# Transposing the second layernorm's output by DMA instead of on TensorE, in a fused cross-attention and FFN kernel

## The reference

```python
def _layernorm(x, axis=-1, eps=1e-05):
    m = jnp.mean(x, axis=axis, keepdims=True)
    v = jnp.var(x, axis=axis, keepdims=True)
    return (x - m) / jnp.sqrt(v + eps)

# xattn(u, ctx): q = Wq u, k = Wk ctx, v = Wv ctx (b, c, positions)
#   softmax(q^T k / sqrt(C)) over the 256 columns, times v, plus Wskip u
# ffn(u): w = (nibbles(qweight) - round(zeros / scales)) * scales, 1024 x 1024
#   y = u @ w + bias
x = x + xattn(_layernorm(x), ctx)        # 32 x 128 x 1024, float32
x = x + ffn(_layernorm(x))               # contraction over the 1024 positions
```

## Time and profile before

| | |
|---|---|
| median of 3 runs | 616.7 us (616.62 to 617.56) |
| the profiled execution's own time | 616.67 us |
| its span, first to last instruction | 614.8 us |
| TensorE busy | 588.1 us (96%) |
| VectorE busy | 476.5 us (77%) |
| GpSimd busy | 468.7 us (76%) |
| ScalarE busy | 409.4 us (67%) |
| granted TensorE clock, mean | 0.989 of full |
| transfers | 41.4 MB, the queue of SyncE 19.7% of 16 engines |

### The profile page before, as it was taken

The page is one execution under the profiler, slowest core; times in us unless marked ns, Lnnn a source line. Parts: engine busy times, 40 slices in busy tenths (PEclk is TensorE's granted clock), DMA queues, the critical chain, the costliest instruction groups (busy, mean ns, idle before and its releaser), DMA issues.

```text
span 614.8 us, 10932 instructions
## 1 busy us (share of the span) xinstructions
PE 588.1 (96%) x3348; PEld 416.1 (68%) x3348; DVE 476.5 (77%) x1027; ACT 409.4 (67%) x976; POOL 468.7 (76%) x520
## 2 busy tenths in 40 slices
PE   2868999999999999999999999999999999999996
PEld 2755777667777766777776677777677777667763
DVE  6787877878887777888778788878777877887762
ACT  4874677666668766666876666686666677666650
POOL 2453788777879877777977787897778789777866
PEclk9977999999999999999999999999999999999999
DMA  8011012222111222211222211122221112221002
GB/s 315 3 43 43 27 53 79 77 77 73 40 53 66 77 77 77 70 41 47 73 77 77 77 65 46 43 77 77 77 77 54 57 43 77 77 77 68 19 19 102
DMA packets 20178, 41.38 MB, mean 67 GB/s; under 512 B 2496, under 2 KB 7104, under 8 KB 20160
## 3 DMA queue, kind: packets, MB, share of 16 engines
q1 hardware_dynamic: 19584, 41.03, 19.7%
q10 hardware_dynamic: 576, 0.14, 0.1%
HBM read 24.39 MB, written 16.78 MB: 67 GB/s over the span
## 4 chain that ended last, share of the span: by engine, by line
PE 91%; DVE 5%; ACT 2%; issue 1%; DMA 1%; POOLq 0%; POOL 0%; ACTq 0%
PE ps_y L676 36%; PE ps_e L610 17%; PE ps_o L644 14%; PE ps_t L625 9%; PE ps_o L637 7%; PE ps_t L657 5%; PE ps_kv L688 2%; PE ps_kv L686 2%; DMA sb_x<-in_x_dram 1%; DVE sb_nib L457 1%; ACT sb_prob L288 1%; DVE sb_pt_lo L408 1%; DVE sb_neg_max L398 0%; ACT sb_pt_hi L297 0%; DVE sb_zp L499 0%
## 5 line engine op out<-in xcount | busy, mean ns | idle before, releaser
L288 ACT ACTIVATE sb_prob<-ps_e,sb_neg_max 128x256 f32<-128x256 f32 x256 | 118.7, 470 | 128.9 <-DVE sb_neg_max L398 128.8
L676 PE MATMUL ps_y<-sb_wf,sb_xnt_hi 128*128 128x512 f16 x512 | 196.1, 383 | 0.9 <-DVE sb_xnt_lo L448 0.9
L676 PE MATMUL ps_y<-sb_wf,sb_xnt_lo 128*128 128x512 f16 x512 | 194.0, 379 | 0.0
L214 POOL TENSOR_SCALAR sb_prob<-sb_prob,sb_rsum 128x256 f32<-128x256 f32 x256 | 117.7, 477 | 27.5 <-DVE sb_rsum L403 27.5
L408 DVE TENSOR_TENSOR sb_pt_lo<-ps_t,sb_pt_hi 128x512 fp32r<-128x512 f32 x128 | 88.3, 691 | 34.6 <-ACT sb_pt_hi L297 30.4
L398 DVE TENSOR_REDUCE sb_neg_max<-ps_e 128x2 f32<-128x512 f32 x128 | 87.7, 686 | 34.8 <-PE ps_e L610 34.8
L610 PE MATMUL ps_e<-sb_kv_hi,sb_xc_hi 128*128 128x256 f32 x256 | 91.6, 358 | 7.7 <-DVE sb_kv_lo L535 4.0
L297 ACT ACTIVATE sb_pt_hi<-ps_t 128x512 fp32r<-128x512 f32 x128 | 76.3, 598 | 33.9 <-PE ps_t L625 33.9
L676 PEld LDWEIGHTS ps_y<-sb_wf,sb_xnt_hi 128*128 128x128 f16 x512 | 49.7, 97 | 59.2 <-issue 17.6
L223 POOL TENSOR_TENSOR sb_rstd<-sb_ve,sb_neg_half 128x1 f32<-128x1 f32 x32 | 17.5, 548 | 92.3 <-DVE sb_ve L443 92.3
L250 POOL TENSOR_TENSOR sb_xc_lo<-sb_xc,sb_xc_hi 128x1024 fp32r<-128x1024 f32 x32 | 76.5, 2390 | 9.2 <-ACT sb_xc_hi L343 7.5
(11 more groups left out here) (85 smaller groups left out, 1162.9 us busy)
## 6 DMA issues: line engine op xcount, KB each, us to landing
sb_x<-in_x_dram SPq DMA_DIRECT2D x32, 512.0 KB, 3.3
out_dram<-sb_o SPq DMA_DIRECT2D x64, 256.0 KB, 2.1
sb_ctx<-in_ctx_dram SPq DMA_DIRECT2D x32, 128.0 KB, 2.5
sb_q<-in_L_ffn_qweight_dram SPq DMA_DIRECT2D x4, 512.0 KB, 6.4
sb_scale_row<-in_L_ffn_scales_dram SPq DMA_DIRECT2D x1, 512.0 KB, 8.7
sb_bias_row<-in_L_ffn_bias_dram SPq DMA_DIRECT2D x1, 512.0 KB, 9.5
sb_wk<-in_L_xattn_Wk_dram SPq DMA_DIRECT2D x1, 64.0 KB, 3.4
sb_wq<-in_L_xattn_Wq_dram SPq DMA_DIRECT2D x1, 64.0 KB, 3.3
```

Of the source, the lines that this page charges most:

```text
L214: last = pool.tensor_scalar(prob[:, j, t, :], prob[:, j, t, :], rsum[:, j, t:t + 1], 1.0, ALU.mult, ALU.mult)
L288: done = act.activation(prob[:, j, t, :], ps_e[j % 2][:, t, :], ACT.Exp, bias=neg_max[:, j, t:t + 1], accum_out=esum[:, j, t:t + 1])
L676: last = pe.matmul(ps_y[h][:, :], xnt_p[s][:, kt, :], wf[:, kt, h * HALF:(h + 1) * HALF], start=kt == 0 and s == 0, stop=kt == KT - 1 and ...
```

## The change

The transposes on TensorE (transpose_xn) are taken out. The split in two fp16 halves is made in SBUF before the transposition: ScalarE copies xn as fp16 to xn_hi with the columns in the order of the blocks (split_xn, one 1024-column instruction after probs_hi(1)), VectorE subtracts it from xn to xn_lo (split_xn_lo, one instruction after probs_lo(1)). SyncE then issues two DMA transposes a batch from SBUF to SBUF, 128 x 1024 fp16 each, into xnt_hi and xnt_lo, which get a second buffer. They stand in SyncE's step behind the stores and before the load of ctx. ffn(p, 0, 0) waits for both; the wait before its third quarter is gone. SyncE's stream is written out in full instead of looped; split_xn and split_xn_lo wait for the transposes of the batch before (xnt_loaded), and the first transpose waits for the FFN of the batch two before (y_done[1]). In the diff, cut to its core, the parts are in this order: buffers, SyncE, ScalarE, VectorE, TensorE; the calls of the removed and added functions follow from the order given above.

```diff
-        xnt_hi, xnt_lo = (sb(n, [P, KT, P], F16) for n in ("xnt_hi", "xnt_lo"))
+        xn_hi, xn_lo = (sb(n, [P, KT, P], F16) for n in ("xn_hi", "xn_lo"))
+        xnt_hi, xnt_lo = (sb(n, [P, 2, KT, P], F16) for n in ("xnt_hi", "xnt_lo"))
...
+                if ran(p):
+                    sp.wait_ge(xnhi_done, p + 1)
+                    if ran(p, 2):
+                        sp.wait_ge(y_done[1], p - 1)
+                    sp.dma_start_transpose(xnt_hi[:, 1 - par, :, :], xn_hi[:, :, :].rearrange(
+                        "c k r -> c (k r)")).then_inc(xnt_loaded[1 - par], 16)
+                    sp.wait_ge(xnlo_done, p + 1)
+                    sp.dma_start_transpose(xnt_lo[:, 1 - par, :, :], xn_lo[:, :, :].rearrange(
+                        "c k r -> c (k r)")).then_inc(xnt_loaded[1 - par], 16)
...
-            def xn_hi(p, h):
-                act.wait_ge(xnt_done[h], p + 1)
-                if h == 0 and ran(p, 1):
-                    act.wait_ge(y_done[1], p)
-                act.activation(xnt_hi[:, 4 * h:4 * h + 4, :], ps_t[h][:, :].rearrange("p (k r) -> p k r", r=P),
-                               ACT.Copy).then_inc(xnthi_done[h], 1)
+            def split_xn(p, par):
+
+                act.wait_ge(xn_done, p + 1)
+                if ran(p, 1):
+                    act.wait_ge(xnt_loaded[1 - par], arrived(p - 1, 1 - par, 32))
+                act.activation(xn_hi[:, :, :].rearrange("c (t e) r -> c t e r", e=2),
+                               xn[:, :].rearrange("c (t r e) -> c t e r", e=2, r=P),
+                               ACT.Copy).then_inc(xnhi_done, 1)
...
+            def split_xn_lo(p, par):
+
+                dve.wait_ge(xnhi_done, p + 1)
+                if ran(p, 1):
+                    dve.wait_ge(xnt_loaded[1 - par], arrived(p - 1, 1 - par, 32))
+                dve.tensor_tensor(xn_lo[:, :, :].rearrange("c (t e) r -> c t e r", e=2),
+                                  xn[:, :].rearrange("c (t r e) -> c t e r", e=2, r=P),
+                                  xn_hi[:, :, :].rearrange("c (t e) r -> c t e r", e=2),
+                                  ALU.subtract).then_inc(xnlo_done, 1)
...
-            def transpose_xn(b, p, h):
-
-                pe.wait_ge(xn_done, p + 1)
...
-                if g == 2 and h == 0:
-                    pe.wait_ge(xntlo_done[1], c + 1)
...
                     if h == 0:
-                        pe.wait_ge(xntlo_done[0], c + 1)
+                        pe.wait_ge(xnt_loaded[cpar], arrived(c, cpar, 32))
```

More of the change, by code:

```diff
@@ L127, in xattn_ffn_program @@
         nb2_done, xn_done = sem("nb2"), sem("xn")
-        xnt_done, xnthi_done, xntlo_done = sems("xnt", HALVES), sems("xnthi", HALVES), sems("xntlo", HALVES)
+        xnhi_done, xnlo_done, xnt_loaded = sem("xnhi"), sem("xnlo"), sems("xnt_loaded", 2)
         zpt_done, addbias_done, rest_done = sem("zpt"), sem("addbias"), sem("rest")
@@ L168, in step @@
             def step(b, par):
-                c = b - 3
+                c, p = b - 3, b - 1
                 if ran(c):
@@ L182, in step @@
                     sp.dma_start(x_sb[:, par, :], x[b + 2, :, :]).then_inc(x_loaded[par], 16)
-            run_steps(sp, step)
+            for b in range(-1, B + 3):
+                step(b, b % 2)
             for par in range(2):
@@ L320, in step @@
                     if ran(p, 1):
-                        act.wait_ge(xnt_done[1], p)
+                        act.wait_ge(xnlo_done, p)
                     act.activation(xn[:, :], x1[:, 1 - par, :], ACT.Identity, bias=nb2[:, :],
@@ L329, in step @@
                     probs_hi(b, 1)
+                if ran(p):
+                    split_xn(p, 1 - par)
                 if isinstance(b, int) and b in (0, 1):
@@ L354, in step @@
                                    scale=rs2[:, :]).then_inc(zpt_done, 1)
-                if ran(p):
-                    xn_hi(p, 0)
-                    xn_hi(p, 1)
                 if ran(n):
@@ L525, in finish @@
                     stats2(b, par, 0)
-                if ran(p):
-                    xn_lo(p, 0)
-                    xn_lo(p, 1)
                 if ran(n):
@@ L573, in step @@
                     probs_lo(b, 1)
+                if ran(p):
+                    split_xn_lo(p, 1 - par)
                 if isinstance(b, int) and b == 1:
@@ L620, in transpose_probs @@
                     pe.wait_ge(ptlo_done[j + 2], b)
-                if j < 2 and ran(b, 2):
-                    pe.wait_ge(xntlo_done[j], b - 1)
                 for m in range(MT):
@@ L646, in attend, with ffn @@
                 last.then_inc(attn_done[h], 1)
-            def transpose_xn(b, p, h):
-                pe.wait_ge(xn_done, p + 1)
-                if ran(b):
-                    pe.wait_ge(ptlo_done[2 + h], b + 1)
-                else:
-                    pe.wait_ge(xntlo_done[h], p)
-                for k in range(4):
-                    t, e = (4 * h + k) // 2, k % 2
-                    last = pe.transpose(ps_t[h][:, k * P:(k + 1) * P],
-                                        xn[:, 2 * P * t + e:2 * P * (t + 1):2], ident[:, :])
-                last.then_inc(xnt_done[h], 1)
-            def ffn(c, h, g):
+            def ffn(c, cpar, h, g):
                 if g == 0:
                     if h == 0:
-                        pe.wait_ge(xntlo_done[0], c + 1)
+                        pe.wait_ge(xnt_loaded[cpar], arrived(c, cpar, 32))
                     if ran(c, 1):
                         pe.wait_ge(prod_done[h], c)
-                if g == 2 and h == 0:
-                    pe.wait_ge(xntlo_done[1], c + 1)
                 if isinstance(c, int) and c == 0 and h == 0:
@@ L675, in ffn @@
                     for s in range(2):
-                        last = pe.matmul(ps_y[h][:, :], xnt_p[s][:, kt, :], wf[:, kt, h * HALF:(h + 1) * HALF],
+                        last = pe.matmul(ps_y[h][:, :], xnt_p[s][:, cpar, kt, :], wf[:, kt, h * HALF:(h + 1) * HALF],
                                          start=kt == 0 and s == 0, stop=kt == KT - 1 and s == 1)
@@ L700, in step @@
                 if ran(q):
-                    ffn(q, 0, 2)
+                    ffn(q, par, 0, 2)
                 if ran(b):
@@ L704, in step @@
                 if ran(q):
-                    ffn(q, 0, 3)
+                    ffn(q, par, 0, 3)
                 if isinstance(b, int) and b == 0:
@@ L710, in step @@
                 if ran(q):
-                    ffn(q, 1, 0)
+                    ffn(q, par, 1, 0)
                 if ran(b):
@@ L716, in step @@
                 if ran(q):
-                    ffn(q, 1, 1)
+                    ffn(q, par, 1, 1)
                 if ran(b):
@@ L720, in step @@
                 if ran(q):
-                    ffn(q, 1, 2)
+                    ffn(q, par, 1, 2)
                 if ran(b):
@@ L725, in step @@
                 if ran(q):
-                    ffn(q, 1, 3)
+                    ffn(q, par, 1, 3)
                 if ran(b):
@@ L732, in step @@
                     keys_values(n, 1 - par)
-                if ran(p):
-                    transpose_xn(b, p, 0)
                 if ran(b):
                     skip(b, par, 1)
-                if ran(p):
-                    transpose_xn(b, p, 1)
                 if ran(b):
@@ L741, in step @@
                 if ran(p):
-                    ffn(p, 0, 0)
-                    ffn(p, 0, 1)
+                    ffn(p, 1 - par, 0, 0)
+                    ffn(p, 1 - par, 0, 1)
             run_steps(pe, step)
```

4 lines of the change are left out of this document (removed).

## The result

The changed kernel takes **695.15 us** (median of 4 runs, 694.37 to 696.36) against 616.66 us for the kernel before: ratio 1.1275, 95% interval 1.1251 to 1.1299. That is 78.5 us slower, where 607 was forecast; the range ended at 690.

What follows compares the result with a forecast made beforehand. TensorE was taken as the bound, busy 588.1 of 614.8 us, with VectorE's queue taking back most of the gain. A step gains 0.06 + 0.27 = 0.33 us: 616.7 - 32 x 0.33 + 1 = 607 us, range 588 to 690.

Steps and rivals of the forecast that it cites:

- Steps 1 and 3: ScalarE's split_xn takes 1.06 us; on VectorE two products, probs_lo(2) and residual(0) queue behind split_xn_lo, until 304.08.
- Step 2: VectorE's split_xn_lo, 1024 columns, takes 1.23 us by a slope per column; bounds 0.7 and 2.3 us.
- Step 4: TensorE's skip(b, 1) starts 0.16 us later, plus 0.25 after the stall, less 0.47: 0.06 us earlier, not 0.94.
- Step 5: Lighter VectorE work behind brings the first row maximum 0.6 us earlier; TensorE's 0.27 us wait for the exponentials goes.
- Step 6: The two DMA transposes, 1.3 us fixed plus 1.1 us service each, land 2.4 us before ffn(b-1, 0, 0) and cost nothing.
- Rivals B and C: Before ffn(b-1, 0, 0): B, transposes land late, 645 us at 3 us service, chance 0.22; C, they bound, 1010 us, 0.12.
- Step 7: On SyncE's queue the context load stands behind the transposes, the x load waits for residual(1); both cost nothing.
- Step 8: In the last batch nothing covers the new path from xn to the products: about +1 us.
- Rival D: On VectorE split_xn_lo takes 2.3 us from its every-other-column read, passed straight to skip(b, 1): 641 us; chance 0.08.
- Rival A: As forecast, VectorE's queue takes back most of the gain: 607 us, its own range 588 to 614; chance 0.47.

Runs made afterwards that it cites:

- e2: The changed kernel with one added wait: GpSimd's bias addition waits until split_xn_lo is done; 609.83 us.
- e6: The changed kernel with 16 matmuls of 256 columns, whose result nobody reads, in TensorE's wait before skip(b, 1); 661.95 us.
- e5: The changed kernel with GpSimd's bias addition waiting for split_xn_lo and VectorE's two FFN products moved behind the first statistics; 605.59 us.
- e7: The changed kernel with GpSimd's bias addition waiting for split_xn_lo, one product ahead of the last row maximum, the other behind the first statistics; 604.94 us.
- e4: The changed kernel with each DMA transpose issued twice, one of them into a spare tile; 700.07 us.
- e1: The changed kernel with both splits taking the columns in plain order instead of every other column; 695.77 us.
- e12: The kernel before, transposes on TensorE, with VectorE's two products spread out and wsk_lo's subtraction moved behind variance2; 608.03 us.

## Why the prediction was wrong

The forecast was 607 us, the result 695. The working, step by step:

- **Steps 1 and 3, the queues: right.** split_xn takes 1141 ns for 1.06 us. From the end of split_xn_lo to x1 the forecast had 304.08 - 301.58 = 2.50 us; in the trace 315.85 to 318.26 is 2.41.
- **Step 2, the price of split_xn_lo: this is the step that failed.** It went by a slope per column, 1.23 us, with bounds of 0.7 and 2.3. The slope was right (1225 ns in e2, all 32 times), but in the changed kernel the instruction takes 2890 on average, above the upper bound, because both bounds came from what VectorE does alone. The rows used for the slope read one input from PSUM and one from SBUF, and the new instruction reads SBUF twice. With whom it would run side by side on GpSimd was never asked.
- **Step 4, the wait at skip(b, 1): place right, size wrong, one term missing.** Forecast was a wait of 0.4 to 0.9 us, 32 times. It is 2.4 us, in every batch; without the hold 0.7, as forecast. The 0.25 us for the stall was right too: skip(b, 1) takes 0.96 us for 0.70 where the clock is kept. What the sum put at nothing, without a reason, is what a longer wait does to TensorE's clock: e6 shows 33 us in all.
- **Step 5, the exponentials: right for this order.** Their wait is one of 3.2 us, and no longer 31; without the hold (e2) it is 5.2 us in 14 times for 18.5 in 31. It comes back when a product stands behind the statistics (19.3 us in e5 and e7).
- **Step 6, the transposes: right, a little dear.** Landing 3.1 us for the 2.4 forecast, SyncE held 1.24 us by each, 3 us to spare. Part of these 3 us is the delay of the reader: without the hold, in e2, the second is issued at 316.31, lands at 319.5 and is read at 321.10, so 1.6 us are left for the 2.4 forecast. The service: q1 took 30.0% of 16 x 693.4 us, against 19.7% of 16 x 614.8 us; the difference over the 67,584 packets that came with the change is 20.6 ns each, for the 17 forecast. They are 1056 a transpose, for 1024 forecast. The 1309 ns for a block in the Trainium skill (page "VectorE: DVE Perf Modes", section "The three transpose paths"), taken eight times, is an estimate of 10.5 us. The trace doesn't agree with that multiplication: eight blocks in one transfer land in 3.1 us. Rivals B and C fall with it, and e4 shows it a second time.
- **Step 7, SyncE's queue: right.** The load of ctx is issued behind the transposes (317.16), the load of x behind residual(1) as before (322.82), and no engine waits for either in the steady steps. VectorE's wait for x even falls, from 14.9 us in 30 times to 4.7 in 2 at the start.
- **Step 8, the end: +1 forecast, +1.6 found.** From the last xn to the last products it was 603.16 - 597.33 = 5.83 us. Now:

```profile
672.74 1.24 ACT L335 ACTIVATE sb_xn<-sb_x,sb_nb,sb_rstd 128x1024 f32<-128x1024 f32 x1 [7.63 <-POOL sb_nb L238]
```

```profile
673.96 1.57 SPq L176 DMA_DIRECT2D out_dram<-sb_o  x2
675.63 1.28 SPq L181 DMA_TRANSPOSE sb_xnt_hi<-sb_xn_hi  x1
676.95 1.33 SPq L184 DMA_TRANSPOSE sb_xnt_lo<-sb_xn_lo  x1
```

with the products from 680.20: 7.46 us. The first transpose is issued 0.4 us late, because two stores stand ahead of it on SyncE (split_xn was done at 675.25, the issue came at 675.63). The second follows at 676.95, 0.44 us after its subtraction is done, and the products start 3.25 us after that issue, where the sum had 2.4.

The sum with what the runs measured: 607 + 32 x 1.66 = 660, where e6 has 662; plus 33 for the clock is 693, and 695.15 was measured.

**Rival D** named the mechanism that decides and its place: split_xn_lo is dear, and each microsecond of it goes straight to skip(b, 1). It had 0.08, because it looked for the cause in the stride, which e1 rules out, and had 2.3 us as its worst. At 2.89 its own rule gives 660 us. Rival A is what the chip does once the hold is taken away: 609.8 measured for 607. (The upper end of its range is a slip: with a third of step 5 the sum is 616.7 - 32 x (0.06 + 0.09) + 1 = 613 and not 614.)

Could it have been seen in the trace of the kernel before? Yes. Its VectorE, in the step of the earlier trace rows, and then its GpSimd:

```profile
306.71 0.58 DVE L531 SCALAR_TENSOR_TENSOR sb_wsk_lo<-sb_proj,sb_rstd,sb_wsk_hi 128x128 fp32r<-128x128 f32 x1 [0.24 <-ACT sb_kv_hi L365]
307.22 0.47 DVE L533 SCALAR_TENSOR_TENSOR sb_kv_lo<-ps_kv,sb_rstd,sb_kv_hi 128x256 fp32r<-128x256 f32 x1
```

```profile
304.75 2.40 POOL L256 TENSOR_TENSOR sb_rest<-sb_rest,sb_zpt 128x1024 f32<-128x1024 f32 x1
```

The same operation takes 0.58 us for 128 columns from SBUF and 0.47 for 256 with one input in PSUM. The first of them ends 0.14 us after GpSimd does, at 307.15. It was the only instruction of the steady state with two SBUF tensors as inputs on VectorE, and it takes 577 ns on average there for the 342 that it takes in e12.

## What to carry to other kernels

Before an operation with two inputs in SBUF is put on VectorE, look at what GpSimd runs at that moment: its price is its own time plus what is left of GpSimd's running SBUF instruction, and everything queued behind it pays too. Where GpSimd has slack, try one wait that makes it go second before any reordering of VectorE; here it turned 695 us into 610, where moving the products alone gave 647. In a trace, look for an instruction whose min and median are far apart (1225 and 2985 ns here), and compare its ends with those of the other engines' instructions; here that found the partner.
